# Attention inside a macaron block on one core: one coarse product in eight copied by ScalarE, and another order of the products

## The reference, cut to what matters

```python
x = x + 0.5 * ffn(layernorm(x))
x = x + attention(layernorm(x))          # 4096 tokens, 16 heads of 16
x = x + 0.5 * ffn(layernorm(x))

def attention(X):
    ctx = X @ We.T                                        # (4096, 32)
    influence = ctx @ ctx.T
    scores = Q @ K.T / 4 + 0.1 * influence                # per head, 4096 x 4096
    return (softmax(scores) @ V).reshape(...) @ Wo.T
```

## Time and profile before

| what | value |
|---|---|
| median of 3 runs | 3822.54 us |
| the profiled execution: its time, its span | 3818.4 us, 3816.6 us |
| TensorE matmul busy | 3681.9 us, 96% |
| VectorE busy | 3112.4 us, 82% |
| ScalarE busy | 2541.6 us, 67% |
| GpSimd busy | 1104.5 us, 29% |
| mean granted clock of TensorE, share of full speed | 0.988 |

### The profile page before, as it was taken

One profiled execution on the slowest core, in us unless ns is written; L12 is line 12 of the kernel. 1 busy time (PEld: TensorE's weight loads), 2 busy tenths in 40 slices (PEclk: granted clock), 3 DMA queues, 4 the chain that ended last, 5 costly groups with the idle time before them and its releaser, 6 DMA issues. The chain is left out here.

```text
span 3816.6 us, 80377 instructions
## 1 busy us (share of the span) xinstructions
PE 3681.9 (96%) x28132; PEld 2181.9 (57%) x28132; DVE 3112.4 (82%) x5241; ACT 2541.6 (67%) x4811; POOL 1104.5 (29%) x906
## 2 busy tenths in 40 slices
PE   3998799999999999999999999999999999999699
PEld 2997455555555555555555555555555555555698
DVE  7996688888888888888888888888888888885798
ACT  4764376666776666677666776666667666667475
POOL 4990112222222222222222222122222222222597
PEclk9999799999999999999999999999999999999899
DMA  3004511212121212121212121212121212122000
GB/s 131 18 20 162 124 38 39 48 39 46 41 48 39 47 40 48 40 48 40 48 40 48 40 49 40 49 40 46 40 47 41 46 41 47 41 50 80 35 19 22
DMA packets 310560, 187.67 MB, mean 49 GB/s; under 512 B 197440, under 2 KB 240864, under 8 KB 309216
## 3 DMA queue, kind: packets, MB, share of 16 engines
q1 hardware_dynamic: 304688, 179.88, 21.3%
q10 hardware_dynamic: 5552, 3.44, 0.4%
HBM read 144.54 MB, written 33.55 MB: 47 GB/s over the span
## 5 line engine op out<-in xcount | busy, mean ns | idle before, releaser
L1310 DVE TENSOR_REDUCE tops<-coarse 128x1 f32<-128x512 f32 x4069 | 2480.5, 681 | 528.3 <-PE coarse L1196 528.1
L1299 ACT ACTIVATE x_all<-fine 128x512 f32<-128x512 f32 x4096 | 2072.1, 598 | 801.6 <-PE fine L1210 801.6
L1210 PE MATMUL fine<-query_a,key_a 64*128 64x512 f32 x4096 | 1554.4, 415 | 0.9 <-DMA query_b<-neg_max 0.9
L1196 PE MATMUL coarse<-key_a,max_query 64*128 64x512 f32 x4069 | 1522.7, 433 | 20.7 <-DMA max_query<-scratch_c_query 13.1
L1210 PE MATMUL fine<-query_c,key_c 64*128 64x512 f32 x4096 | 1517.5, 406 | 0.6 <-ACT x_all L1299 0.3
L1210 PE MATMUL fine<-query_b,key_b 33*128 33x512 f32 x4096 | 1468.4, 394 | 0.0
L1196 PEld LDWEIGHTS coarse<-key_a,max_query 64*128 64x128 f32 x4069 | 716.0, 186 | 606.8 <-DVE tops L1310 359.8
L1219 PE MATMUL o_ps<-x_all,vh 128*32 128x512 f32 x8192 | 984.7, 598 | 0.0
L1210 PEld LDWEIGHTS fine<-query_a,key_a 64*128 64x128 f32 x4096 | 749.1, 184 | 211.3 <-issue 129.5
L1210 PEld LDWEIGHTS fine<-query_b,key_b 33*128 33x128 f32 x4096 | 755.8, 185 | 75.5
L1210 PEld LDWEIGHTS fine<-query_c,key_c 64*128 64x128 f32 x4096 | 736.1, 185 | 99.9 <-ACT x_all L1299 10.8
(11 more groups left out here) (193 smaller groups left out, 2649.5 us busy)
## 6 DMA issues: line engine op xcount, KB each, us to landing
query_c<-scratch_c_query SPq DMA_DIRECT2D x256, 128.0 KB, 2.7
query_a<-scratch_q_hi SPq DMA_DIRECT2D x512, 32.0 KB, 1.8
query_a<-scratch_c_query SPq DMA_DIRECT2D x256, 64.0 KB, 2.0
query_b<-neg_max SPq DMA_DIRECT2D x1024, 0.5 KB, 2.0
max_query<-scratch_q_hi SPq DMA_DIRECT2D x508, 32.0 KB, 1.8
max_query<-scratch_c_query SPq DMA_DIRECT2D x254, 64.0 KB, 2.0
query_b<-scratch_q_lo SPq DMA_DIRECT2D x256, 32.0 KB, 2.4
x_all<-in_L_attn_X SPq DMA_DIRECT2D x4, 1024.0 KB, 12.4
```

Of the source, the lines that this page charges most:

```text
L1196: return pe.matmul(bank, max_query[n][half_rows(r, 0, HALF), q * P:(q + 1) * P], key_a[keys][half_rows(r, 0, HALF), kb * 512:(kb + 1) * 51 ...
L1210: return pe.matmul(fine[i % 2][:, r, :], keys[rows, cols], query[rows, :], start=chunk == 0, stop=chunk == CHUNKS - 1)
L1299: act.activation(probs[:, i % RING, r, :], fine[i % 2][:, r, :], ACT.Exp).then_inc(probs_ready, 1)
L1310: dve.tensor_reduce(tops[n][:, idx // KB, idx % KB:idx % KB + 1], bank, AX.X, ALU.max).then_inc(tops_ready, 1)
```

## The change

It has three parts. (1) The table `WAVES` gets new strings. (2) The coarse product number 4 of each group (`VIA_ACT`) is copied by ScalarE from its bank to one of two buffers `spare` in SBUF. VectorE reduces the buffer and waits for `copied`. TensorE waits for `copied`, and not for the reduction, before it writes product number 7 into that bank. (3) ScalarE's order of work (`ACT_EVENTS`) gets the copy at the place where the product stands in the table, between e3 and e4.

```diff
-WAVES = ["CCfffCfffCffffff", "fffCffffffCfffCC"]
+WAVES = ["CfCfffffCffCffff", "ffffCffffCffffCC"]
+VIA_ACT = 4
...
                 wave.append((r, None, products[r], count))
                 products[r] += 1
+                if count == VIA_ACT:
+                    events.append(None)
                 count += 1
...
+        spare = [sb(f"spare{n}", [P, 512]) for n in range(2)]
...
+        def copy_number(t, idx):
+            return (UNITS * t + idx - UNITS - AHEAD) // UNITS_IN_GROUP
+        def is_copied(t, idx):
+            return idx % UNITS_IN_GROUP == VIA_ACT and UNITS * t + idx >= UNITS + AHEAD
+        def coarse_bank(t, idx):
+            return coarse[(UNITS * t + idx) % COARSE][:, :]
...
-                    pe.wait_ge(tops_ready, UNITS * t + idx - COARSE + 1)
+                    if idx >= COARSE and is_copied(t, idx - COARSE):
+                        pe.wait_ge(copied, copy_number(t, idx - COARSE) + 1)
+                    else:
+                        pe.wait_ge(tops_ready, UNITS * t + idx - COARSE + 1)
...
+                def copy_coarse(s, g):
+                    step, idx = divmod(AHEAD + UNITS_IN_GROUP * g + VIA_ACT, UNITS)
+                    t = s + 1 + step
+                    if within(t):
+                        n = copy_number(t, idx)
+                        act.wait_ge(coarse_ready, UNITS * t + idx + 1)
+                        act.wait_ge(tops_ready, UNITS * t + idx - 2 * UNITS_IN_GROUP + 1)
+                        act.activation(spare[n % 2][:, :], coarse_bank(t, idx), ACT.Copy).then_inc(copied, 1)
...
-                        for e, (tile, r) in enumerate(TILES_ENDED):
-                            i = GROUP * g + tile
-                            act.wait_ge(fine_ready, TILES * s + TILES_IN_GROUP * g + e + 1)
-                            act.activation(probs[:, i % RING, r, :], fine[i % 2][:, r, :], ACT.Exp).then_inc(probs_ready, 1)
-                            if g == 0 and e == SUMS_AFTER and s > 0:
-                                take_sums(s - 1)
+                        e = 0
+                        for event in ACT_EVENTS:
+                            if event is None:
+                                copy_coarse(s, g)
+                            else:
+                                tile, r = event
+                                i = GROUP * g + tile
+                                act.wait_ge(fine_ready, TILES * s + TILES_IN_GROUP * g + e + 1)
+                                act.activation(probs[:, i % RING, r, :], fine[i % 2][:, r, :], ACT.Exp).then_inc(probs_ready, 1)
+                                e += 1
+                        if g == 0 and s > 0:
+                            take_sums(s - 1)
...
-                    dve.wait_ge(coarse_ready, UNITS * t + idx + 1)
+                    if is_copied(t, idx):
+                        dve.wait_ge(copied, copy_number(t, idx) + 1)
+                    else:
+                        dve.wait_ge(coarse_ready, UNITS * t + idx + 1)
...
-                        reduce_max(t, t % 2, idx, coarse[(UNITS * t + idx) % COARSE][:, :])
+                        reduce_max(t, t % 2, idx, spare[copy_number(t, idx) % 2][:, :] if is_copied(t, idx) else coarse_bank(t, idx))
```

More of the change, by code:

```diff
@@ L897 @@
 AHEAD = 16
-WAVES = ["CCfffCfffCffffff", "fffCffffffCfffCC"]
+WAVES = ["CfCfffffCffCffff", "ffffCffffCffffCC"]
+VIA_ACT = 4
 CHUNKS = 3
 def group_of_waves():
-    waves, tiles, products, ended = [], [0, 0], [0, 0], []
+    waves, tiles, products, events = [], [0, 0], [0, 0], []
     count = 0
@@ L918, in group_of_waves @@
                 if chunk == CHUNKS - 1:
-                    ended.append((tile, r))
+                    events.append((tile, r))
         waves.append(wave)
-    return waves, ended
-GROUP_WAVES, TILES_ENDED = group_of_waves()
+    return waves, events
+GROUP_WAVES, ACT_EVENTS = group_of_waves()
+TILES_ENDED = [event for event in ACT_EVENTS if event is not None]
 UNITS_IN_GROUP = len(WAVES[0]) * 2 - 2 * GROUP * CHUNKS
 TILES_IN_GROUP = 2 * GROUP
-SUMS_AFTER = TILES_IN_GROUP - 1
 INVERT_AFTER = 7
@@ L1036, in attention_phase @@
         fine_ready, probs_ready, pv_done = sem("fine_ready"), sem("probs_ready"), sem("pv_done")
-        coarse_ready, tops_ready, neg_ready = sem("coarse_ready"), sem("tops_ready"), sem("neg_ready")
+        coarse_ready, copied, tops_ready, neg_ready = sem("coarse_ready"), sem("copied"), sem("tops_ready"), sem("neg_ready")
         TILES = 2 * PAIRS
@@ L1256, in body @@
                                 if tile is None and within(t):
-                                    coarse_product(coarse[(UNITS * t + unit % UNITS + order) % COARSE][:, :], n, keys, unit % UNITS // KB, r, what).then_inc(coarse_ready, 1)
+                                    coarse_product(coarse_bank(t, unit % UNITS + order), n, keys, unit % UNITS // KB, r, what).then_inc(coarse_ready, 1)
                                 elif tile is not None:
```

## The result

| | kernel before | with the change |
|---|---|---|
| median, 20 runs each | 3819.72 us (3815.61 to 3825.86) | 3825.76 us (3822.74 to 3832.49) |
| ratio to before | | 1.0017, 95% interval 1.001 to 1.0024 |
| profiled execution: time, span | 3818.4, 3816.6 us | 3825.03, 3823.2 us |

The change costs 6 us where 10 us were forecast to be gained. By the prediction's bound of 0.2% this counts as no difference, though the interval lies wholly above 1. The measured time lies inside the stated range (3794 to 3842), but it moved the other way. In the unit of the prediction the miss is 16 us, or 0.03 us a group. Three single executions of the first batch of experiments (12250.28 us in e1, 4832.37 and 7099.24 us of the kernel before) were far slower than all others, and no median or ratio here contains them.

What follows compares the result with a forecast made beforehand. TensorE, 96% busy, was taken as the bound, losing time to VectorE waits. -0.21 + 0.07 + 0.03 + 0.09 = -0.02 us a group, times 512 = -10 us: profiled 3808, median 3812 us, range 3794 to 3842.

Steps and rivals of the forecast that it cites:

- Two losses of VectorE: TensorE's waves 5 and 10 wait for VectorE's reductions, losing 0.11 and 0.10 us; the new order removes both, -0.21 a group.
- (a): Price from the releasing operation's end to TensorE's weight load where the wave has one wait: 0.05 us.
- (b): Price from releasing operation to weight load where a wave has two waits and the later-placed ends last: 0.12 us.
- (c): Price of a late weight load on TensorE: its wave starts 0.10 us later.
- The chain e0, e1, e2: ScalarE's first three exponentials hold waves 7, 9, 11, costing 0.07, 0.03, 0.09 us; nearly all of 0.21 is asked back.
- rival A: The exponentials' chain eats the whole gain if the third follows the second at 0.50: 3818 to 3823 us, chance 0.28.
- e0 does not move, since w2 does not.: ScalarE's first exponential in a group keeps its start, because the wave completing its tile keeps its time: no shift.
- The copy hides with 0.04 to spare: ScalarE's copy ends at 10.29, so C7 may run at 10.44, before the last wave is due at 10.48.
- its second wait costs little: The copy's two waits on ScalarE are both long satisfied; the second costs 0.03 us, within bounds of 0 and 0.07.
- Rival B: The copied product becomes the wait that ends last, delaying the group's last wave: slower, 3838 to 3858 us, chance 0.24.
- VectorE's slack is 0.4: Waiting for the copy shrinks VectorE's slack from 0.9 to 0.4 us a group, and its once-a-step operations still fit.
- a w15 later than 3.83 after w0: Sign in the timeline: the group's last wave over 3.83 us after its first would mean the copy delays it.

Runs made afterwards that it cites:

- e1: The changed kernel with the matmul that ends the first exponential's tile issued ahead of coarse product C1 in wave 2: 3812.47 us, ratio 0.9982 to the kernel before.
- e2: The kernel before with the copy of coarse product 4 by ScalarE alone, its table of waves unchanged: 3821.95 us, ratio 1.0005.
- e4: The changed kernel with the wait on exponentials written first where a wave has two waits: 3807.51 us, ratio 0.9969 to the kernel before.
- e3: The changed kernel without the copy, so only the new order of waves: 3881.73 us, ratio 1.0161 to the kernel before.
- e7: The kernel before with only another table of waves, nothing copied and waits written as there: 3793.75 us, ratio 0.9935.
- e6: The changed kernel with wave 2's matmuls swapped, exponentials' wait first, C3 in wave 7 instead of 8, no copy: 3790.84 us, ratio 0.9932 to the kernel before.

## Why the prediction was wrong

- **Two losses of VectorE go, 0.21.** Right: gone in the changed kernel, back in e2.
- **Prices (a) 0.05, (b) 0.12, (c) 0.10.** Right. In the changed kernel e0 ends at 11.05 and w7's load is at 11.10, which is (a). w8 follows at 11.44, so w7 ran at 11.21, 0.11 after its load, against 0.10 for (c). e4 shows (b) by taking it away.
- **The chain e0, e1, e2 fixes w11, and gives nearly all back.** Right. e2 follows e1 by 0.48, so rival A's distance of 0.50 was not what happened. The time came out within A's 0.2%, but not by A's mechanism, and A's own sum was 0 to -0.01 where the group grew by 0.006.
- **"e0 does not move, since w2 does not."** This is the step that failed. w2 did not move, e0 did, by 0.027. The step looked at when the matmul ends and not at what ends with it. C1 had moved into w2, in the other half of the array and first in the order of issue. 0.027 x 512 is 14 us of the 16 missed; e1 took it out and gained 13. With it out, the prediction's sum was sound: the group of e1 is 0.021 shorter than before against the 0.02 forecast, and the whole -7 us against -10.
- **The copy hides with 0.04 to spare, its second wait costs little.** Right: the copy starts 0.48 after e3, the ordinary distance, C7's load follows the copy's end (13.00) at 13.06, and w15 follows w14 by one wave. Rival B's price was not paid. e2 shows that the copy costs nothing, e3 that the new order needs it.
- **VectorE's slack is 0.4 and suffices; SBUF is no faster to reduce.** Right: its waits are 0.47 for the copy and 0.39 at C0, and 0.69 against 0.68.

Two of the prediction's own signs need a word. It made a w15 later than 3.83 after w0 the sign of rival B, and w15 stands at 3.84. The sign could not carry that: it says that w15 is late, not that the copy made it so. And it gave 2.86 to 2.89 after w0 for the weight load at w11; by its own working that is the wave, and the load was due at 2.76. It came at 2.78, late by e0.

Where the 6 us lie is known in part. The median group is 0.006 longer, 3 us in all. Another 2 us lie in single long groups, the first of a step, where w2 waits for the maxima: these waits add up to 1.6 us in the trace before and 3.6 us in the changed one. The later `neg_max` alone does not explain them. They are 1.8 us in e2, which has the copy, and 5.5 us in e7, which has none. Their cause stays open.

## What to carry to other kernels

When two matmuls run side by side and both signal, put the one first whose reader is on the path. Where an instruction has two waits, write first the one that ends last; at w11 that brought the load 0.07 us forward and the group 0.04. After removing a wait, follow the next chain through every link, down to the order within a pair: two swaps of this size (31 us) decided the sign of a change whose two large terms, 0.21 and 0.19, nearly cancelled. And ask of an added operation which gap it mends: closing that gap by the order alone (e6) did the same without it.

## What the runs showed of the hardware

- A matmul that signals behind another of the same wave is seen 0.027 us later by its reader (e0 at 1.09 and 1.06 after w0, changed kernel and e1; medians 1.091 and 1.062). The issue itself differs by 0.01. That the two signals take turns was not measured by itself. The Trainium skill (TensorE: Matmul & The Clock Gate, "The cost: per-tile semaphore tail") says that increments of concurrent tiles serialize, at 26.3 ns each; the 0.027 here agrees in size.
- With two waits on one matmul, the wait that the program writes last costs 0.12 from the releasing operation's end to the weight load, the one written first 0.05 (e4 against the changed kernel, w11, behind ScalarE; w10 of the kernel before shows the 0.12 behind VectorE, 9.08 to 9.20).
- ScalarE starts an operation of 512 elements every 0.48 us when it is never idle, whether exponential or copy (the first distance of a group, e0 to e1, is 0.49 to 0.50), while the recorded length of one grows from 0.60 to 0.68 over the nine of a group (medians of the changed kernel). By the Trainium skill (ScalarE: Activation LUTs, "What ACT_TABLE_LOAD costs"), 186 ns + 0.833 ns an element less an overlap of 93 ns, the estimate is 0.52; the rows here decide for 0.48.
